# Two edits around a four-layer convolution kernel: zeros stored in long runs at the opening, and another order of loads and stores in layer 3

## What is computed

```
x = x + L0(gn(x))   # 1x1 conv to 576 channels, depthwise 3x3, 5x5 and 7x7,
                    # 1x1 conv, channel attention with top-k softmax, 1x1 conv
x = x + L1(gn(x))   # channel attention
x = x + L2(gn(x))   # selective scan
x = x + L3(gn(x))   # depthwise 7x7 conv with mirrored borders, plus bias
```

## Time and profile before

| | us |
|---|---|
| median of 3 runs | 2481.89 |
| the profiled execution's own time | 2484.08 |
| its span, first to last instruction | 2482.2 |
| TensorE busy | 1941.6 (78%) |
| VectorE busy | 1276.3 (51%) |
| GpSimd busy | 856.1 (34%) |
| ScalarE busy | 804.2 (32%) |

### The profile page before, as it was taken

The page is one execution under the profiler, slowest core; times in us unless marked ns, Lnnn a source line. Parts: engine busy times, 40 slices in busy tenths (PEclk is TensorE's granted clock), DMA queues, the critical chain, the costliest instruction groups (busy, mean ns, idle before and its releaser), DMA issues. The chain is left out here.

```text
span 2482.2 us, 36929 instructions
## 1 busy us (share of the span) xinstructions
PE 1941.6 (78%) x15660; PEld 1208.7 (49%) x15660; DVE 1276.3 (51%) x1317; ACT 804.2 (32%) x1269; POOL 856.1 (34%) x452
## 2 busy tenths in 40 slices
PE   3789899769999999999977867777677767775042
PEld 1477776667777777777734422222222222221032
DVE  5445454441111111111172055799999999998613
ACT  2345455440000000000042125733543444334610
POOL 3234333430000000000000040499899989994000
PEclk9889899889999999999988878899889988998565
DMA  8899999969242323221030031588778868873799
GB/s 292 264 347 318 345 326 345 357 214 242 63 117 62 105 75 93 87 82 39 1 102 11 0 116 44 133 204 213 183 198 221 214 163 220 210 187 108 206 293 309
DMA packets 205013, 441.32 MB, mean 178 GB/s; under 512 B 19728, under 2 KB 150800, under 8 KB 192432
## 3 DMA queue, kind: packets, MB, share of 16 engines
q1 hardware_dynamic: 180976, 426.47, 57.9%
q10 hardware_dynamic: 23872, 12.49, 1.8%
HBM read 309.65 MB, written 128.45 MB: 176 GB/s over the span
## 5 line engine op out<-in xcount | busy, mean ns | idle before, releaser
L755 PE MATMUL ps<-mem 128*128 128x288 f16 x5376 | 654.8, 287 | 9.6 <-DMA mem<-depthwise_out 9.6
L755 PEld LDWEIGHTS ps<-mem 128*128 128x128 f16 x5376 | 502.1, 98 | 148.2 <-issue 15.4
L1729 POOL TENSOR_TENSOR mem<-mem 128x1024 f32<-128x1024 f32 x192 | 465.5, 2441 | 45.3 <-ACT mem L1663 42.7
L1638 PE MATMUL ps<-mem 128*128 128x512 f32 x768 | 416.6, 675 | 39.4 <-POOL mem L1729 35.6
L540 PE MATMUL ps<-mem 56*96 56x240 f16 (+1 forms) x5184 | 314.8, 284 | 74.3 <-POOL mem L630 41.1
L1124 POOL TENSOR_TENSOR mem<-mem 128x1536 f16<-128x1536 f32 x16 | 50.8, 3179 | 928.7 <-ACT mem L1102 928.7
L540 PEld LDWEIGHTS ps<-mem 56*96 56x96 f16 x5184 | 305.4, 131 | 98.8 <-issue 56.6
L798 DVE TENSOR_TENSOR mem<-ps,mem 128x128 f16<-128x128 f32 x64 | 18.7, 292 | 586.9 <-ACT mem L819 586.9
L1758 DVE TENSOR_TENSOR_SCAN mem<-mem,ps 128x1024 f32<-128x1024 f32 x132 | 307.8, 2332 | 18.2 <-issue 10.3
L654 DVE TENSOR_TENSOR mem<-ps,mem 96x1024 f16<-96x1024 f32 x144 | 175.5, 1221 | 212.4 <-ACT mem L585 212.3
L1638 PEld LDWEIGHTS ps<-mem 128*128 128x128 f32 x768 | 153.5, 213 | 242.7 <-issue 133.7
(11 more groups left out here) (201 smaller groups left out, 1883.9 us busy)
## 6 DMA issues: line engine op xcount, KB each, us to landing
mem<-l_bc SPq DMA_DIRECT2D x504, 256.0 KB, 4.5
depthwise_out<-mem SPq DMA_DIRECT2D x35, 1536.0 KB, 10.8
mem<-depthwise_out SPq DMA_DIRECT2D x95, 512.0 KB, 6.2
mem<-base_phases SPq DMA_DIRECT2D x36, 1024.0 KB, 12.8
base_phases<-mem SPq DMA_DIRECT2D x112, 256.0 KB, 6.5
mem<-in_wd SPq DMA_DIRECT2D x36, 768.0 KB, 14.2
mem<-l_planes SPq DMA_DIRECT2D x12, 1152.0 KB, 8.4
mem<-depthwise_out SPq DMA_DIRECT2D x128, 64.0 KB, 6.0
```

The costliest lines, as they stand in the source:

```text
L755: ins = nc.tensor.matmul(ps[:, 2 * (i % 2) + h, 0:HALF], d, pw[rows, wa, k, HALF * h:HALF * h + HALF], start=(k == 0 and n == 0), stop=(k ...
L1638: ins = nc.tensor.matmul(py[:, a, :], ident, hh[:, n % 4, 512 * a:512 * a + 512], start=(n % N == 0), stop=(n % N == N - 1))
L1729: nc.gpsimd.tensor_tensor(hh[:, n % 4, :], hh[:, n % 4, :], cs[:, n % 4, :], ALU.mult).then_inc(hc_pool, 1)
```

## The change

At the opening, the rows of zeros are contiguous in DRAM, so each DRAM region is written as 128 long runs, one from each partition: four stores in place of eight, of the same bytes. In layer 3 the float32 taps get a third buffer (the three are as large as the three windows, and window s goes to buffer (s + 1) % 3, so each window has to wait only for the piece that lay there). Pieces 0 to 2 load in the norm's block, piece 3 as soon as piece 0 is split, which is now the first thing ACT and DVE do. Tile 2's first half is stored after window 3 in place of before it, and ACT issues tile 2's second half after its first copy out of PSUM. ACT's stores of tile 0 and 1 stand between two normalising instructions of the next tile. PE waits for each piece of taps when it comes to it.

```diff
@@ layer0_depthwise, first_loads @@
-    def store_unused(sp, t):
-        size = B * 2 * PLANE
-        src = ext[0:C // 2].rearrange("c s r n -> c (s r n)")[:, 0:(64 - TAPROWS) * size].rearrange("c (r n) -> c r n", n=size)
-        sp.dma_start(planes_d[t, TAPROWS:64].rearrange("r c b n -> c r (b n)"), src).then_inc(sem.unused_planes, 16)
+    def store_unused(sp, dst, done):
+        dst = dst.rearrange("(p n) -> p n", p=128)
+        sp.dma_start(dst, ext.rearrange("p s r n -> p (s r n)")[:, 0:dst.shape[1]]).then_inc(done, 16)
...
         for t in range(2):
-            for k in range(3):
-                sp.dma_start(base_d[t, TAPROWS:64, 96 * k:96 * k + 96].rearrange("r c n -> c r n"),
-                             ext[0:96, 0:2].rearrange("c a r n -> c (a r) n")).then_inc(rest_stored, 16)
-            store_unused(sp, t)
+            store_unused(sp, base_d[t, TAPROWS:64].rearrange("r c n -> (r c n)"), rest_stored)
+            store_unused(sp, planes_d[t, TAPROWS:64].rearrange("r c b n -> (r c b n)"), sem.unused_planes)
@@ layer3 @@
-    w32 = [ar.take(3 * WC) for _ in range(2)]
+    w32 = [ar.take(3 * WC) for _ in range(3)]
...
     def first_taps(sp):
-        for i in range(2):
+        for i in range(3):
             load_taps(sp, i)
@@ layer3, SP @@
+            sp.wait_ge(tap_lo, 1)
+            load_taps(sp, 3)
+            sp.wait_ge(rows_done, 1)
+            store_planes(sp, 0, 0)
+            sp.wait_ge(rows_done, 2)
+            store_planes(sp, 1, 0)
+            sp.wait_ge(sem.unused_planes, 32)
             for t in range(2):
-                sp.wait_ge(rows_done, t + 1)
-                store_planes(sp, t, 0)
-                sp.wait_ge(tap_hi, t + 1)
-                sp.wait_ge(tap_lo, t + 1)
-                load_taps(sp, t + 2)
-            sp.wait_ge(tap_hi, NPIECE)
-            sp.wait_ge(tap_lo, NPIECE)
-            sp.wait_ge(sem.unused_planes, 32)
-            sp.wait_ge(stored[0], used + 32)
-            sp.wait_ge(stored[1], used + 32)
-            for n in range(NW):
-                load_windows(n)
-            sp.wait_ge(rows_done, NT)
+                sp.wait_ge(stored[t], used + 32)
+            for s in range(NW):
+                sp.wait_ge(tap_lo, min(s + 2, NPIECE))
+                load_windows(s)
+            load_windows(NW)          # waits for conv_sum >= 1
+            sp.wait_ge(rows_done, 3)
             store_planes(sp, 2, 0)
@@ layer3, PE @@
-                if n == 0:
-                    pe.wait_ge(tap_hi, NPIECE)
-                    pe.wait_ge(tap_lo, NPIECE)
+                if n % 3 == 0:
+                    pe.wait_ge(tap_hi, n // 3 + 1)
+                    pe.wait_ge(tap_lo, n // 3 + 1)
@@ layer3, ACT @@
-            normalise(0)
             taps(0)
+            normalise(0, range(4))
+            taps(1)
             shift_right(0)
-            normalise(1)
+            normalise(1, (0, 1))
             store_second(0)
-            taps(1)
+            normalise(1, (2, 3))
+            taps(2)
             shift_right(1)
-            taps(2)
+            taps(3)
+            normalise(2, (0, 1))
             store_second(1)
-            normalise(2)
-            taps(3)
+            normalise(2, (2, 3))
             shift_right(2)
-            store_second(2)
             for n in range(NB3):
...
                 act.wait_ge(conv_out, n + 1)
+                if n == 0:
+                    store_second(2)
@@ layer3, DVE @@
+            taps(0)
             for t in range(NT):
...
-                if t == 2:
-                    taps(3)
...
-                for i in ((0,), (1, 2), ())[t]:
+                for i in ((1,), (2, 3), ())[t]:
                     taps(i)
```

More of the change, by code:

```diff
@@ L473, in _ @@
             wait_stored(0)
-            sp.wait_ge(rest_stored, 96)
+            sp.wait_ge(rest_stored, 32)
             for n in range(2):
@@ L632, in _ @@
             split_taps(0)
-            pool.wait_ge(rest_stored, 96)
+            pool.wait_ge(rest_stored, 32)
             pool.wait_ge(sem.unused_planes, 32)
@@ L1815, in layer3 @@
     ar.at = at
-    w32 = [ar.take(3 * WC) for _ in range(2)]
-    ar.at = max(ar.at, end)
+    w32 = [ar.take(3 * WC) for _ in range(3)]
+    assert ar.at <= end
+    ar.at = end
     at = ar.at
@@ L1825, in layer3 @@
     used = sem.shifted[1]
-    tap_in = sem.shifted[0][3:5]
+    tap_in = sem.shifted[0][3:6]
     tap_hi = sem("l3_taps_high_part")
@@ L1845, in layer3, with slot @@
     out_stored = sem("l3_out_stored")
+    def slot(s):
+        return (s + 1) % NW
     def main_rows(t, r, a):
@@ L1874, in load_taps @@
     def load_taps(sp, i):
-        sp.dma_start(w32[i % 2], inp["wd3"][:, 3 * WC * i:3 * WC * (i + 1)]).then_inc(tap_in[i % 2], 16)
+        sp.dma_start(w32[i % 3], inp["wd3"][:, 3 * WC * i:3 * WC * (i + 1)]).then_inc(tap_in[i % 3], 16)
     def store_planes(eng, t, h):
@@ L1899, in _ @@
             sp.dma_start(bias, inp["b3"]).then_inc(bias_in, 16)
-            def load_windows(n):
-                src = planes_d.rearrange("t f c b n -> (t f) c (b n)")[:, BP * n:BP * n + BP]
-                sp.dma_start(win[:, n % NW], src).then_inc(win_in[n % NW], 16)
-            for t in range(2):
-                sp.wait_ge(rows_done, t + 1)
-                store_planes(sp, t, 0)
-                sp.wait_ge(tap_hi, t + 1)
-                sp.wait_ge(tap_lo, t + 1)
-                load_taps(sp, t + 2)
@@ L1910, in _, with load_windows @@
-            sp.wait_ge(tap_hi, NPIECE)
-            sp.wait_ge(tap_lo, NPIECE)
-            sp.wait_ge(sem.unused_planes, 32)
-            sp.wait_ge(stored[0], used + 32)
-            sp.wait_ge(stored[1], used + 32)
-            for n in range(NW):
-                load_windows(n)
-            sp.wait_ge(rows_done, NT)
+            def load_windows(s):
+                if s >= NW:
+                    sp.wait_ge(conv_sum, s - NW + 1)
+                src = planes_d.rearrange("t f c b n -> (t f) c (b n)")[:, BP * s:BP * s + BP]
+                sp.dma_start(win[:, slot(s)], src).then_inc(win_in[slot(s)], 16)
@@ new lines, in load_sums, with store_out @@
+            def load_sums(t):
+                for p0, b, c0, n in pieces(t):
+                    sp.dma_start(cv[p0:p0 + n, t], conv_d[b, c0:c0 + n]).then_inc(conv_in[t], 16)
+            def store_out(i):
+                for h in range(2):
+                    s = slice(HW // 2 * h, HW // 2 * (h + 1))
+                    sp.wait_ge(added, 8 * i + 4 * h + 4)
+                    for p0, b, c0, n in pieces(i):
+                        sp.dma_start(xout[b, c0:c0 + n, s], xt[p0:p0 + n, i, s]).then_inc(out_stored, 16)
@@ L1918, in _ @@
             store_planes(sp, 2, 0)
-            for n in range(NW, NB3):
-                sp.wait_ge(conv_sum, n - NW + 1)
-                if CB * n == 128:
+            for s in range(NW + 1, NB3):
+                if CB * s == 128:
                     sp.wait_ge(stored[2], used + 64)
-                load_windows(n)
+                load_windows(s)
             for k in range(NSTG):
                 sp.wait_ge(conv_stored[k], 64 * (128 // CB // NSTG))
-            sp.wait_ge(stored[2], used + 64)
@@ L1927, in _ @@
-            for t in range(NT):
-                if t == 2:
[L1929 to L1938, removed]
+            for t in range(2):
+                load_sums(t)
@@ L1939, in _ @@
+            for k in range(NSTG):
+                sp.wait_ge(conv_stored[k], 64 * (NB3 // NSTG))
+            load_sums(2)
+            for i in range(NT):
+                store_out(i)
             sp.wait_ge(out_stored, 128)
@@ L1943, in _ @@
             for n in range(NB3):
-                pe.wait_ge(win_in[n % NW], win_base[n % NW] + 16 * (n // NW + 1))
-                if n == 0:
-                    pe.wait_ge(tap_hi, NPIECE)
-                    pe.wait_ge(tap_lo, NPIECE)
+                pe.wait_ge(win_in[slot(n)], win_base[slot(n)] + 16 * (n // NW + 1))
+                if n % 3 == 0:
+                    pe.wait_ge(tap_hi, n // 3 + 1)
+                    pe.wait_ge(tap_lo, n // 3 + 1)
                 if n >= 4:
@@ L1954, in _ @@
                                 for t in range(2):
-                                    x = win[64 * t:64 * t + TAPROWS, n % NW, 4 * h + j].rearrange("p (b h n) -> p b h n", b=B, h=2)
+                                    x = win[64 * t:64 * t + TAPROWS, slot(n), 4 * h + j].rearrange("p (b h n) -> p b h n", b=B, h=2)
                                     out = ps[M3 * j:M3 * j + M3, bank(n) + t, 256 * h:256 * h + 256].rearrange("p (b n) -> p b n", b=B)
@@ L1963, in _, with normalise @@
         def _(act):
[L1964 to L1967, removed]
+            def normalise(i, rows):
+                t = i
+                for r in rows:
+                    if i:
+                        act.wait_ge(x_lo, 4 * i - 3 + r)
                     nc.scalar.activation(phase_rows(r).rearrange("p f (y x) -> p f y x", x=8), natural(xt[:, t], r), ACT.Identity,
```

(28 more changed lines are left out.)

## The result

The changed kernel took 2470.20 us (median of 6 runs, 2463.18 to 2477.11), the kernel before beside it 2484.44 (6 runs, 2481.09 to 2492.42). The ratio is 0.9939, 95% interval 0.9915 to 0.9963: 14 us or 0.6% faster. The forecast was 15.9 us. A second set of runs gave 0.9926 (0.9898 to 0.9953).

What follows compares the result with a forecast made beforehand. The main block was taken to wait for SP's issuing of zeros, and the convolution to be bound by bytes; the opening's -11.4 us and layer 3's -4.5 sum to -15.9, giving 2466.0 us, range 2460 to 2475.

Steps and rivals of the forecast that it cites:

- SP's issuing (step 1 of the opening): Opening: SP's four zero stores issued by 23.8 us, under the norm's 29.55; main block starts at 30.0, 11.4 us earlier.
- The zeros (step 2): Opening: long runs of zeros move at 430 GB/s and land at some 42 us; at 275 GB/s, 49.5.
- What waits (step 3): Opening: POOL waits some 3 us for zeros and catches up; the shift reaches the end, -11.4 us, bounds -4 and -11.4.
- First plane store and tile 1 (steps 1 and 2 of layer 3): Layer 3: SP's first plane store 2.2 us later; taps ready 19.5 us earlier; ACT's halves issued later than SP's.
- Those stores (step 3): Layer 3: tiles 0 and 1 stored at about 2352, bounds 2349 and 2356, so windows issued 5.7 us earlier.
- Tile 2's store (step 5): Layer 3: store ends at the same time, 2388, but window 3 goes ahead of it; -4.5 us, bounds 0 and -7.7.
- The opening gives little: Rival, opening: long zeros no faster, or SP's issuing still waits for each transfer to land; 2473.4 us, chance 0.20.
- Slower: Rival, layer 3: tile 2's planes move slower ahead of window 4, holding steps from 4 on; 2491 us, chance 0.06.
- Full rates in layer 3: Rival, layer 3: both halves together reach 303 GB/s, windows issued at 2349; 2462.8 us, chance 0.15.

Runs made afterwards that it cites:

- e7: The changed kernel storing the long runs of zeros a second time, to a spare tensor (6.49 MB more); ratio to the kernel before 0.9984.
- e3: The changed kernel run a second time, with nothing altered, beside the kernel before; ratio 0.9926.
- e1: The kernel before with only the opening's zeros in long runs, layer 3 left as before; ratio to the kernel before 0.9952.
- e5: The changed kernel with ACT storing the two parts of tile 2's second half in the other order, partitions 96 to 127 first; ratio to the kernel before 0.9894.
- e6: The changed kernel with tile 2's store moved back, before window 3 on SP and before the first copy on ACT; ratio to the kernel before 0.9921.
- e11: e6 with ACT's two parts of tile 2's second half in the other order; ratio to the kernel before 0.9921.
- e2: The kernel before with only layer 3 changed, the opening's zeros left as before; ratio to the kernel before 0.9974.
- e10: The changed kernel with only ACT's half of tile 2's store back before its first copy, SP's still after window 3; ratio to the kernel before 0.9885.
- e8: The changed kernel with tiles 0 and 1 stored in DMAs of 32 partitions, four a tile in place of two; ratio to the kernel before 0.9937.

## Why the prediction came out as it did

**SP's issuing (step 1 of the opening): right.** The block starts at 29.98 (forecast 30.0). The four stores were issued by 15.5, not 23.8: the bound of 3.7 us each was too wide, and harmless.

**The zeros (step 2): right.** 430 GB/s and a landing at 42; measured 407 to 448 and 41.6. At the lower bound, the old rate, they would have landed at 49.5, and by the estimate beside e7 some 5 of the 13 us would have been left.

**What waits (step 3): right, slightly low.** The term was -11.4. The first depthwise matmul is 13.1, 12.7 and 11.6 us earlier than 88.0 in the changed kernel, e3 and e1; over all nine runs with the long zeros it comes at 74.9 to 77.2, where the three with short ones have 86.9 to 88.7, 12 us earlier in the mean. e1's whole time is 11.9 lower.

**First plane store and tile 1 (steps 1 and 2 of layer 3): the sizes right, the stagger wrong.** SP's first store comes 25.0 us after the norm's first vector instruction, 22.9 before: 2.1 later, forecast 2.2. I took ACT's halves to be issued after the normalising instructions ahead of them. They are not:

```profile
2300.04 2.25 ACT L1976 ACTIVATE mem<-mem 128x1024 f32<-128x1024 f32 x1
2301.64 0.69 ACTq L1882 DMA_DIRECT2D l_planes<-mem  x1
2302.18 6.55 ACT L1976 ACTIVATE mem<-mem 128x1024 f32<-128x1024 f32 x3
```

This is the timeline of the changed kernel; SP's half is issued at 2301.64 as well. Both activations stand ahead of ACT's store in its list. The one of 2300.04 runs until 2302.29, the next hasn't begun, and the queue has issued the DMA by then: a DMA's issue waits for its semaphore, not for the compute instruction ahead of it. The kernel before shows the same, in a row that I hadn't read:

```profile
2316.56 0.69 ACTq L1881 DMA_DIRECT2D l_planes<-mem  x1
2317.10 6.55 ACT L1968 ACTIVATE mem<-mem 128x1024 f32<-128x1024 f32 x3
```

Its `store_second(0)` stands behind all four instructions of `normalise(1)`, three of which begin after the issue. What does hold an issue is a semaphore that the list waits for ahead of it: tile 1's second half went out at 2336.89 there, when the taps that ACT's next cast waits for had landed (2336.88). In the changed kernel no such wait is left, and tile 1's halves are issued together too, both at 2315.50.

**Those stores (step 3): the time right, from a wrong cause.** Windows were forecast 5.7 us earlier and came 4.6 to 5.4 earlier. I had SP alone for 4.5 us and again for 3, because ACT would issue late. ACT issues at once; one queue does run alone, but because the other's packets come late, by some 3 us for tile 0 and 6 for tile 1. That the two sum to nearly the same time is luck. Windows of the changed kernel: SP's queue alone, both, then ACT's queue alone between the tiles (all 1294 packets are its own):

```profile
2303.00:2305.00 2.00, 0.00 (x0) 0.00 (x0) 1.97 (x3) 2.00 (x2) 0.00 (x0) 0.50 0.81 175
2308.00:2315.00 7.00, 0.00 (x0) 0.00 (x0) 6.79 (x14) 6.17 (x4) 0.00 (x0) 0.50 1.09 301
2317.00:2321.00 4.00, 0.00 (x0) 0.00 (x0) 3.52 (x3) 4.00 (x3) 0.00 (x0) 0.50 0.80 184
```

One half alone moves at 175 to 184 GB/s, both at 301, and SP's half of tile 1, issued at 2315.50, has not begun by 2321. My 303 for both halves is borne out by that 301.

The Trainium skill's page "SBUF — State Buffer", section "Door 1: The DMA port swizzle", gives partitions 0 to 63 the ports of 0 to 31; the changed kernel, e5, e6 and e11 agree with it, for the pairs within one 64 run at 195 and 212 GB/s and the pairs across at 293 and 309. The page's section "Can I just issue two DMAs to hit both halves?", by which two such DMAs gain only 6%, is not borne out here, for stores in runs of 576 B from two queues: 175 against 301.

**Tile 2's store (step 5): the size of the sum nearly right, a part of its reasoning wrong.** The term for layer 3 was -4.5. Measured were 5.5 between the means, and 6.5 in e2's comparison. Window 4 landed 100.0 us after the norm, where window 3 had landed after 101.2, as forecast ("it ends at the same time"). PE's wait for it, forecast at 20 us or more, was 11.75: steps 0 to 3 took 23.7 us (2341.22 to 2364.89), where I had 3.6 each. But the value of moving the store, one window's bytes, doesn't show: e6 without the move is as fast. With the taps out of the way the old place lets ACT use idle time and puts the two queues out of step, which I had not seen. What is left for layer 3's gain is the taps, loaded in idle time and split early, by which every run with the new order issues its windows 4.6 us or more sooner; no run changes the taps alone.

**The rivals.** "The opening gives little" fell with SP's four short issues and the landing at 41.6. "Slower" fell: window 4 landed at 100.0, far from its deciding point. "Full rates in layer 3" fell, for the windows came no earlier than I had them; the 5 us that e5 found lay elsewhere, in tile 2's rate.

Open: why a queue's packets begin 3 to 6 us late beside a full other queue, what e10's ratio comes from, and what makes the depthwise stage of layer 0 vary by 16 us from run to run.

## What to carry to other kernels

Look at what an engine waits for at a block's boundary: here it was SP still issuing stores of short runs, while every engine that computes had been done for 11 us. Write constants as long runs from all partitions, and check both ends of such an edit, the issue and the landing. When two queues store halves of a tile, pair the partitions so that one is in 0 to 63 while the other is in 64 to 127; the order of two DMAs was worth 5 us.

## What the runs showed of the hardware that was not expected

- Two queues in the same half of the partitions move 195 GB/s together, hardly more than one queue alone on 64 partitions (175 to 184) or on 32 (185 in e6); 0 to 31 with 96 to 127 gives 293 (runs of 576 B).
- What the same order of DMAs does depends on when each queue starts: 293 GB/s in e5, 212 in a window of e11, where the other order had 309 (e6).
- With both queues' stores issued in the same tenth of a microsecond (2315.50), the one behind a full queue of the other side began to move only after 2321; in e8, with DMAs of half the size, it moved 1 us after its issue.
- ACT issues a DMA while its own activation ahead of it in program order still runs and the next one ahead has not begun (issue at 2301.64, activations until 2302.29 and from 2302.18). A semaphore wait ahead of it does hold it (2336.89 in the kernel before).
